# Cross-attention's row maxima: one instruction over two PSUM banks and one shift a head, in place of two of each

## The chip, the cores and the metric

One core of one Trainium2 chip runs the whole program. The metric is the device time of one execution in microseconds (us); the kernel before took 717.56 us, the median of three runs (717.15 to 718.02).

## The reference

Four batches of 256 tokens by 128 features, and a context of 512 rows by 256 features for each. The program is a cross-attention block followed by a transformer layer with a mixture of experts:

```
x = x + layernorm(xattn(layernorm(x), ctx)) ;  x = x + ffn_layer(layernorm(x))

xattn: q = x Wq (16 heads of 64);  k, v = split(ctx Wkv);  one learned null key and value put in front
       sim = (q / 8) k^T          per head: 256 queries x (512 keys + the null key)
       attn = softmax(sim);  out = (attn v) Wout, layernormed
ffn_layer: causal self-attention (16 heads of 8, 8 kv heads), then 8 experts of 448 hidden, top 2
```

The softmax takes each row's maximum over 512 scores and the null score, and subtracts it before the exponential. The change is to how that maximum and the shift made of it are computed.

## The kernel before, in words

**Stages.** `load_and_split` (to about 36 us of the trace), `cross_attention` (to about 395 us), then the residual, self-attention, routing and experts. Only `cross_attention` is touched. float32 products are made of three (or two) fp32r matmuls of high and low parts, so each tile that a matmul reads is rounded by ScalarE (the head) and has its remainder taken by VectorE (the tail).

**Tiling.** A head has two query tiles of 128 rows (t = 0, 1) against 512 keys, so one tile's scores are 128x512 float32 and fill one PSUM bank; tile t goes to `s_bank[t]`. There are 4 batches of 16 heads, 64 heads in all.

**Order.** Each engine has its own hand-written `steps(b, which)`. A step h works on several heads at once, in a software pipeline. FIRST (steps -4 to 1) fills it; BODY (steps 2 to 17) runs in a hardware loop three times, and once more, unrolled, for the last batch. In step h:

- VectorE (`steps`, L610): maximum of head h+2, tile 0 (L582); the q tail of head h+3 (L577); the shift of tile 0 (L587); the maximum and shift of tile 1; two tails of the transposed probabilities of head h (L606); the tails of the step's projection units (L122, L125 and L126, L129); the reciprocal of the sum (L592); the o tail (L598).
- ScalarE (L537): q head (L510), two heads of transposed probabilities (L534), a unit in `q_whole` if there is one (L107 to L112), the two exponentials of head h+2 (L516), the unit in `proj_bank`, the null exponential (L521), the o head (L527).
- TensorE (L479): eight transposes (L439), the units (L94, L96 or L87), `weighted_values` of h-1 (L451), `project_out` of h-2 (L460), `project_q` of h+4 (L414), `scores` of h+3 (L426).
- GpSimd (L645): d0, the total, p0 and the two normalised tiles `p_norm` (L657) of each head.

**Projection units.** The keys and values of a head pair or a token tile are projected just in time. `AT` (L357) gives each step its units: a key unit ("k": two tails of 64x512 on VectorE), a value unit ("v": one tail) or a context transpose ("c"). In each batch step 7 has a key unit in `q_whole` and a value unit in `proj_bank`; step 16 the same for the next batch; step 10 has the two context units, the first in `q_whole`. `q_whole` is the bank that q is projected into, so its unit waits for the step's q tail (L398).

**Waits that the change touches.** `scores` raises `s_ps` once a tile and waits until the exponential of the same tile of the head before is done (L424). `maximum(b, h, t)` waits for its own tile of scores (L581), `shift` for the maximum (L586), and `exponential` for its tile's shift through `bias_s` (L513). GpSimd's d0 waits for both shifts (L646). In the loop the waited values and the column of `s0n` (`null_score`, L367) depend on the loop's register.

Of the kernel before, what the change touches and what calls it, by code (L numbers as in the profile page):

```python
# [20 lines left out]
P = 128  # L21
# [293 lines left out]
def cross_attention(nc, k, dram):  # L315

    with ExitStack() as ctx:
# [20 lines left out]
        banks = [bank(f"bank{i}") for i in range(8)]  # L338
# [56 lines left out]
        def _(pe):  # L395
# [22 lines left out]
            def scores(b, h):  # L418
                pe.wait_ge(q_lo_s, b * H + h + 1)
                if h % 2 == 0:  # L420
                    pe.wait_ge(k.proj_lo, (b + h // H) * NU + UNITS.index(("k", h % H // 2)) + 1)
                for t in range(QT):
                    if h >= 1:
                        pe.wait_ge(p_exp, b * H * QT + QT * (h - 1) + t + 1)  # L424
                    for i, q in enumerate((q_hi, q_lo)):
                        last = pe.matmul(s_bank[t][:, :], q[:, h % 2, t * P:(t + 1) * P], keys[:, h % H, :],  # L426
                                         start=i == 0, stop=i == 1)
                    last.then_inc(s_ps, 1)
# [76 lines left out]
        def _(act):  # L505
# [6 lines left out]
            def exponential(b, h, t):  # L512
                act.wait_ge(bias_s, b * H * QT + QT * h + t + 1)  # L513
                if h >= 2:
                    act.wait_ge(p_norm_s, b * H * QT + QT * (h - 2) + t + 1)
                act.activation(p_raw[:, h % 2, t, :], s_bank[t][:, :], ACT.Exp,  # L516
                               bias=bias[:, h % H, t:t + 1], scale=X_SCALE, accum_out=row_sum[:, h % H, t:t + 1]).then_inc(p_exp, 1)
# [54 lines left out]
        def _(dve):  # L572
# [7 lines left out]
            def maximum(b, h, t):  # L580
                dve.wait_ge(s_ps, b * H * QT + QT * h + t + 1)  # L581
                dve.tensor_reduce(neg_max[:, h % H, t:t + 1], s_bank[t][:, :], AX_X, ALU.max, negate=True).then_inc(max_s, 1)  # L582

            def shift(b, h, t):

                dve.wait_ge(max_s, b * H * QT + QT * h + t + 1)  # L586
                dve.scalar_tensor_tensor(bias[:, h % H, t:t + 1], neg_max[:, h % H, t:t + 1], X_SCALE, null_score(b, h, t),  # L587
# [22 lines left out]
            def steps(b, which, last_batch=False):  # L610
                end = H if last_batch else which.stop + 3
                for h in which:
                    if 0 <= h + 2 < end:
                        maximum(b, h + 2, 0)
                    if 0 <= h + 3 < end:
                        q_tail(b, h + 3)
                    if 0 <= h + 2 < end:
                        shift(b, h + 2, 0)
                        maximum(b, h + 2, 1)
                        shift(b, h + 2, 1)  # L620
# [23 lines left out]
        def _(pool):  # L644
            def normalise_probs(b, h):  # L645
                pool.wait_ge(bias_s, b * H * QT + QT * (h + 1))  # L646
# [968 lines left out]
```

## Time and profile before

| what | value |
|---|---|
| timed runs: median (range) | 717.56 us (717.15 to 718.02) |
| profiled execution: span from first to last instruction | 711.4 us |
| its own time outside the span | not on the page; the span is 6.2 us under the timed median |
| cross-attention in the trace | 36 to 395 us |
| PE, PEld busy | 602.2 us (85%), 492.3 us (69%) |
| DVE (VectorE) busy | 587.9 us (83%), 1282 instructions |
| ACT (ScalarE) busy | 454.6 us (64%) |
| POOL (GpSimd) busy | 227.9 us (32%) |
| TensorE's granted clock, mean | 0.956 |

Busy shares are over the whole span. In the loop of cross-attention VectorE and TensorE are both close to nine tenths busy, so the shares alone don't say which waits decide; the chain of starts within one step does. A row of a timeline gives start, duration, engine, line, operation, and in brackets the idle time before it and who ended it. Instructions of one engine overlap a little (a 0.68 us reduction is followed by the next start 0.60 us later), so distances from start to start are used below.

### The profile page before, as it was taken

The page shows a single profiled execution, that of the slowest core. Times are in us where ns is not written, and L with a number is a line of the kernel's source. Part 1 is how long each engine was busy: PE and PEld are TensorE (multiplying, and loading weights), DVE is VectorE, ACT ScalarE, POOL GpSimd, SP SyncE. Part 2 cuts the span into 40 slices and gives each one's busy share as a digit, 9 for nine tenths or more (in the row PEclk, how much of TensorE's full clock was granted, in tenths as well). Part 3 has the DMA queues.
Part 4 walks back from the last instruction along what each step waited for, and adds up shares of the span by engine and source line. Part 5 has one row for each costly group of instructions (what it writes and reads, how often), then busy time and mean ns, then how long its engine had stood idle before and what let it go on. Part 6 is the DMA issues. An engine that isn't in the chain of part 4 may idle for free. (4 is left out here: it accounts for less than half of the span.)

```text
span 711.4 us, 13311 instructions
## 1 busy us (share of the span) xinstructions
PE 602.2 (85%) x3580; PEld 492.3 (69%) x3580; DVE 587.9 (83%) x1282; ACT 454.6 (64%) x1094; POOL 227.9 (32%) x435
## 2 busy tenths in 40 slices
PE   2979889988999999899999336899997689797996
PEld 2757778767887778778787325666666577575885
DVE  4768899878898788998889747899983599979995
ACT  3657777766777677767777125888883356344563
POOL 1553334323333333333335354722132321414000
PEclk9989999999999999999999868999998699998999
DMA  8020000000000000000000002000000220200000
GB/s 255 17 54 2 2 29 3 1 1 0 0 30 0 1 0 0 0 0 1 1 1 1 1 4 82 1 1 0 0 0 1 78 77 2 77 1 0 0 0 29
DMA packets 15342, 13.48 MB, mean 19 GB/s; under 512 B 1984, under 2 KB 14656, under 8 KB 15296
## 3 DMA queue, kind: packets, MB, share of 16 engines
q1 hardware_dynamic: 15072, 12.94, 6.2%
q8 instruction: 16, 0.26, 0.2%
q14 instruction: 30, 0.25, 0.1%
q10 hardware_dynamic: 224, 0.03, 0.0%
HBM read 12.44 MB, written 0.52 MB: 18 GB/s over the span
## 5 line engine op out<-in xcount | busy, mean ns | idle before, releaser
L516 ACT ACTIVATE p_raw<-bank,bias 128x512 f32<-128x512 f32 x128 | 87.7, 688 | 43.1 <-DVE bias L587 39.4
L582 DVE TENSOR_REDUCE neg_max<-bank 128x1 f32<-128x512 f32 x128 | 86.9, 679 | 5.9 <-issue 4.0
L657 POOL TENSOR_SCALAR p_norm<-p_raw,rinv 128x512 f32<-128x512 f32 x128 | 87.0, 692 | 0.1
L606 DVE TENSOR_TENSOR pT_lo<-bank,pT_hi 128x512 fp32r<-128x512 f32 x128 | 82.4, 685 | 3.9 <-issue 2.3
L534 ACT ACTIVATE pT_hi<-bank 128x512 fp32r<-128x512 f32 x128 | 69.7, 599 | 24.9 <-PE bank L439 23.4
L1472 ACT ACTIVATE act_hi<-act_f 128x512 fp32r<-128x512 f32 x56 | 35.4, 632 | 58.9 <-DVE act_f L1515 58.8
L439 PE MATMUL bank<-ident,p_norm 128*128 128x128 f32 x512 | 66.8, 273 | 0.4 <-DVE pT_lo L606 0.4
L439 PEld LDWEIGHTS bank<-ident,p_norm 128*128 128x128 f32 x512 | 59.8, 141 | 9.3 <-issue 1.2
L451 PE MATMUL bank<-pT_hi,vals 128*128 128x256 f32 x256 | 64.9, 286 | 1.5 <-DVE o_lo L598 1.5
L451 PE MATMUL bank<-pT_lo,vals 128*128 128x256 f32 x256 | 64.0, 283 | 0.0
L426 PE MATMUL bank<-keys,q_hi 128*128 128x512 f32 x128 | 54.7, 427 | 3.0 <-ACT p_raw L516 2.8
L426 PE MATMUL bank<-keys,q_lo 128*128 128x512 f32 x128 | 51.4, 401 | 0.0
L451 PEld LDWEIGHTS bank<-pT_hi,vals 128*128 128x128 f32 x256 | 48.4, 189 | 4.2 <-issue 1.1
L451 PEld LDWEIGHTS bank<-pT_lo,vals 128*128 128x128 f32 x256 | 48.6, 190 | 2.1
L1519 DVE TENSOR_TENSOR act_lo<-act_f,act_hi 128x512 fp32r<-128x512 f32 x56 | 47.2, 842 | 2.7 <-ACT act_hi L1472 1.4
L587 DVE SCALAR_TENSOR_TENSOR bias<-neg_max,s0n 128x1 f32<-128x1 f32 x128 | 41.5, 324 | 7.9 <-DVE neg_max L582 1.9
L650 POOL TENSOR_TENSOR total<-row_sum,e 128x2 f32<-128x2 f32 x64 | 12.5, 195 | 103.4 <-ACT e L521 103.4
L1515 DVE TENSOR_TENSOR act_f<-up_w,gate 128x512 f32<-128x512 f32 x56 | 45.2, 808 | 0.3
L1044 ACT ACTIVATE p_raw<-s_pair,neg_max 128x128 f32<-128x128 f32 (+1 forms) x128 | 43.0, 427 | 3.0 <-DVE neg_max L1109 3.0
L1507 DVE TENSOR_TENSOR up_w<-u_bank,wide 128x512 f32<-128x512 f32 x48 | 33.1, 689 | 8.8 <-PE u_bank L1420 7.4
L1109 DVE TENSOR_REDUCE neg_max<-s_pair 128x2 f32<-128x256 f32 x64 | 32.3, 545 | 5.7 <-PE s_pair L948 5.6
L1428 PE MATMUL d_bank<-act_hi,dn_hi 128*128 128x512 f32 x56 | 23.7, 423 | 15.3 <-DVE act_lo L1519 15.3
(272 smaller groups left out, 1731.3 us busy)
## 6 DMA issues: line engine op xcount, KB each, us to landing
ctx_raw<-in_ctx SPq DMA_DIRECT2D x4, 512.0 KB, 4.7
wkv_raw<-in_L_xattn_Wkv SPq DMA_DIRECT2D x2, 1024.0 KB, 11.1
gu_raw<-in_L_ffn_w_gate SPq DMA_DIRECT2D x4, 448.0 KB, 3.6
gu_raw<-in_L_ffn_w_up SPq DMA_DIRECT2D x4, 448.0 KB, 4.3
dn_raw<-in_L_ffn_w_down SPq DMA_DIRECT2D x4, 448.0 KB, 5.1
wout_raw<-in_L_xattn_Wout SPq DMA_DIRECT2D x2, 512.0 KB, 14.8
x<-in_x SPq DMA_DIRECT2D x1, 512.0 KB, 6.8
wq_raw<-in_L_xattn_Wq SPq DMA_DIRECT2D x1, 512.0 KB, 10.2
```

Source lines behind the costliest of these rows:

```text
L426: last = pe.matmul(s_bank[t][:, :], q[:, h % 2, t * P:(t + 1) * P], keys[:, h % H, :], start=i == 0, stop=i == 1)
L439: last = pe.transpose(t_bank[half][:, j * N + t * P:j * N + (t + 1) * P], p_norm[:, h % 2, t, kt * P:(kt + 1) * P], k.ident[:, :])
L451: last = pe.matmul(o_bank, vals[:, kt, h % H, :], x[:, h % 2, kt, :], start=kt == 0 and i == 0, stop=kt == KT - 1 and i == 1)
L516: act.activation(p_raw[:, h % 2, t, :], s_bank[t][:, :], ACT.Exp, bias=bias[:, h % H, t:t + 1], scale=X_SCALE, accum_out=row_sum[:, h % H, ...
L534: act.activation(pT_hi[:, h % 2, 2 * half:2 * half + 2, :], t_bank[half][:, :].rearrange("p (j n) -> p j n", j=2), ACT.Copy).then_inc(t_hi ...
L582: dve.tensor_reduce(neg_max[:, h % H, t:t + 1], s_bank[t][:, :], AX_X, ALU.max, negate=True).then_inc(max_s, 1)
L587: dve.scalar_tensor_tensor(bias[:, h % H, t:t + 1], neg_max[:, h % H, t:t + 1], X_SCALE, null_score(b, h, t), ALU.mult, ALU.min).then_inc( ...
L606: dve.tensor_tensor(pT_lo[:, h % 2, 2 * half:2 * half + 2, :], t_bank[half][:, :].rearrange("p (j n) -> p j n", j=2), f(pT_hi[:, h % 2, 2 ...
L657: pool.tensor_scalar(p_norm[:, h % 2, t, :], p_raw[:, h % 2, t, :], rinv[:, h % H, t:t + 1], 1.0, ALU.mult, ALU.mult).then_inc(p_norm_s, 1)
L1044: last = act.activation(p_raw[:, p % 4, j, t, 0:n], s_bank[(p % 2) * REP + j][:, t * N:t * N + n], ACT.Exp, bias=neg_max[:, t, REP * (p % ...
L1515: dve.tensor_tensor(act_f[:, n % 2, :], up_w[:, n % 2, :], gate[:, n % 2, :], ALU.mult).then_inc(mul_s, 1)
L1519: dve.tensor_tensor(act_lo[:, n % 2, :], act_f[:, n % 2, :], f(act_hi[:, n % 2, :]), ALU.subtract).then_inc(a_lo_s, 1)
```

## The change

The two score banks become one PSUM tensor `s_both` of 128 x 2 x 512, with `s_bank[t]` a view of each half. `maximum` reads both halves in one TENSOR_REDUCE with two outputs a partition and waits for both tiles' scores; one `shift` makes both biases; `max_s` and `bias_s` count heads instead of tiles. The q tail stays between maximum and shift.

```diff
-        banks = [bank(f"bank{i}") for i in range(8)]
+        s_both = ctx.enter_context(nc.psum_tensor("s_both", [P, QT, BANK], F32))
+        banks = [s_both[:, t, :] for t in range(QT)] + [bank(f"bank{i}") for i in range(2, 8)]
...
             def exponential(b, h, t):
-                act.wait_ge(bias_s, b * H * QT + QT * h + t + 1)
+                act.wait_ge(bias_s, b * H + h + 1)
...
-            def maximum(b, h, t):
-                dve.wait_ge(s_ps, b * H * QT + QT * h + t + 1)
-                dve.tensor_reduce(neg_max[:, h % H, t:t + 1], s_bank[t][:, :], AX_X, ALU.max, negate=True).then_inc(max_s, 1)
-
-            def shift(b, h, t):
-
-                dve.wait_ge(max_s, b * H * QT + QT * h + t + 1)
-                dve.scalar_tensor_tensor(bias[:, h % H, t:t + 1], neg_max[:, h % H, t:t + 1], X_SCALE, null_score(b, h, t),
+            def maximum(b, h):
+                dve.wait_ge(s_ps, b * H * QT + QT * (h + 1))
+                dve.tensor_reduce(neg_max[:, h % H, :], s_both[:, :, :], AX_X, ALU.max, negate=True).then_inc(max_s, 1)
+
+            def shift(b, h):
+
+                dve.wait_ge(max_s, b * H + h + 1)
+                dve.scalar_tensor_tensor(bias[:, h % H, :], neg_max[:, h % H, :], X_SCALE, null_score(b, h, 0, QT),
                                          ALU.mult, ALU.min).then_inc(bias_s, 1)
...
                     if 0 <= h + 2 < end:
-                        maximum(b, h + 2, 0)
+                        maximum(b, h + 2)
                     if 0 <= h + 3 < end:
                         q_tail(b, h + 3)
                     if 0 <= h + 2 < end:
-                        shift(b, h + 2, 0)
-                        maximum(b, h + 2, 1)
-                        shift(b, h + 2, 1)
+                        shift(b, h + 2)
...
             def normalise_probs(b, h):
-                pool.wait_ge(bias_s, b * H * QT + QT * (h + 1))
+                pool.wait_ge(bias_s, b * H + h + 1)
```

## Rows read from the trace of the kernel before

**Rows 1.** The page's costliest groups: busy, mean ns, idle before.

```profile
L582 DVE TENSOR_REDUCE neg_max<-bank 128x1 f32<-128x512 f32 x128 | 86.9, 679 | 5.9 <-issue 4.0
L587 DVE SCALAR_TENSOR_TENSOR bias<-neg_max,s0n 128x1 f32<-128x1 f32 x128 | 41.5, 324 | 7.9 <-DVE neg_max L582 1.9
```

**Rows 2.** Busy time by stretch, second loop iteration: PE, PEld, DVE, ACT, POOL, clock, DMA.

```profile
147.10:239.10 92.00, 83.44 (x525) 71.12 (x524) 80.32 (x172) 66.79 (x173) 30.75 (x80) 1.00 0.02 6
```

**Rows 3.** The waits, 60 to 400 us: total us, times, longest.

```profile
ACT p_raw L516 <- DVE bias L587: 35.3, 35, 1.6
...
DVE keys L125 <- ACT keys L110: 17.2, 29, 0.9
...
PE bank L94 <- DVE q_lo L577: 7.0, 7, 1.2
...
PE bank L87 <- DVE q_lo L577: 4.8, 3, 1.6
```

**Rows 4.** Timeline, all engines: from a maximum after a key unit to the next step's.

```profile
204.98 0.68 DVE L582 TENSOR_REDUCE neg_max<-bank 128x1 f32<-128x512 f32 x1
...
207.32 0.69 ACT L516 ACTIVATE p_raw<-bank,bias 128x512 f32<-128x512 f32 x1
...
208.62 0.69 DVE L129 TENSOR_TENSOR vals<-bank,vals 128x512 fp32r<-128x512 f32 x1
...
209.62 0.68 DVE L582 TENSOR_REDUCE neg_max<-bank 128x1 f32<-128x512 f32 x1
...
209.78 1.36 POOL L657 TENSOR_SCALAR p_norm<-p_raw,rinv 128x512 f32<-128x512 f32 x2
...
210.22 0.41 DVE L577 TENSOR_TENSOR q_lo<-bank,q_hi 128x256 fp32r<-128x256 f32 x1
...
210.55 0.60 DVE L587 SCALAR_TENSOR_TENSOR bias<-neg_max,s0n 128x1 f32<-128x1 f32 x1
...
211.18 0.69 ACT L516 ACTIVATE p_raw<-bank,bias 128x512 f32<-128x512 f32 x1 [0.74 <-DVE bias L587]
...
212.09 0.69 ACT L516 ACTIVATE p_raw<-bank,bias 128x512 f32<-128x512 f32 x1
```

**Rows 5.** Groups by shape: the self-attention's maxima, two outputs a partition.

```profile
L1109 DVE TENSOR_REDUCE neg_max<-s_pair 128x2 f32<-128x512 f32 x32 | 21.6, 675 | 0.0
...
L1109 DVE TENSOR_REDUCE neg_max<-s_pair 128x2 f32<-128x256 f32 x32 | 13.3, 414 | 5.7 <-PE s_pair L948 5.6
```

**Rows 6.** Timeline, back-to-back exponentials, after a unit in q_whole.

```profile
200.47 0.69 ACT L516 ACTIVATE p_raw<-bank,bias 128x512 f32<-128x512 f32 x1
...
201.13 0.70 ACT L516 ACTIVATE p_raw<-bank,bias 128x512 f32<-128x512 f32 x1
```

**Rows 7.** Timeline of a step with a key unit in q_whole (step 7).

```profile
175.76 0.41 DVE L577 TENSOR_TENSOR q_lo<-bank,q_hi 128x256 fp32r<-128x256 f32 x1
...
176.22 0.50 PE L94 MATMUL bank<-cT_hi,wkv_hi 128*128 128x512 f32 x1 [1.20 <-DVE q_lo L577]
...
177.92 0.59 ACT L109 ACTIVATE keys<-bank 64x512 fp32r<-64x512 f32 x1 [2.21 <-PE bank L94]
```

**Rows 8.** Timeline at the loop's turn, GpSimd quiet.

```profile
147.11 0.69 DVE L582 TENSOR_REDUCE neg_max<-bank 128x1 f32<-128x512 f32 x1 [2.13 <-issue]
...
148.05 0.15 DVE L587 SCALAR_TENSOR_TENSOR bias<-neg_max,s0n 128x1 f32<-128x1 f32 x1
...
149.24 0.69 ACT L516 ACTIVATE p_raw<-bank,bias 128x512 f32<-128x512 f32 x1 [0.15 <-DVE bias L587]
```

**Rows 9.** Timeline in the unrolled last batch, after a key step.

```profile
352.08 0.68 DVE L582 TENSOR_REDUCE neg_max<-bank 128x1 f32<-128x512 f32 x1
...
354.21 0.69 ACT L516 ACTIVATE p_raw<-bank,bias 128x512 f32<-128x512 f32 x1
```

**Rows 10.** Timeline of the first head's maximum.

```profile
39.03 0.69 DVE L582 TENSOR_REDUCE neg_max<-bank 128x1 f32<-128x512 f32 x1 [1.83 <-PE bank L426]
39.22 0.63 PE L426 MATMUL bank<-keys,q_lo 128*128 128x512 f32 x1
```

More of the change, by code:

```diff
@@ L425, in scores @@
                     for i, q in enumerate((q_hi, q_lo)):
-                        last = pe.matmul(s_bank[t][:, :], q[:, h % 2, t * P:(t + 1) * P], keys[:, h % H, :],
+                        last = pe.matmul(s_bank[t], q[:, h % 2, t * P:(t + 1) * P], keys[:, h % H, :],
                                          start=i == 0, stop=i == 1)
@@ L512, in exponential @@
             def exponential(b, h, t):
-                act.wait_ge(bias_s, b * H * QT + QT * h + t + 1)
+                act.wait_ge(bias_s, b * H + h + 1)
                 if h >= 2:
                     act.wait_ge(p_norm_s, b * H * QT + QT * (h - 2) + t + 1)
-                act.activation(p_raw[:, h % 2, t, :], s_bank[t][:, :], ACT.Exp,
+                act.activation(p_raw[:, h % 2, t, :], s_bank[t], ACT.Exp,
                                bias=bias[:, h % H, t:t + 1], scale=X_SCALE, accum_out=row_sum[:, h % H, t:t + 1]).then_inc(p_exp, 1)
```

## The prediction, made before the changed kernel was run

> **What bounds the kernel now.** I read the page's costliest groups first [rows 1]: 128 reductions of 679 ns and 128 shifts of 324 ns, a tiny operation that should not take that long. Then the busy time by stretch [rows 2]: in a loop iteration of 92.0 us VectorE is busy for 80.3 and TensorE for 83.4, so neither has much room. Then the waits [rows 3], which say more: VectorE itself waits 17.2 us in 29 key steps for ScalarE's rounding of the keys, and ScalarE waits 35.3 us for the bias. The two engines hand the work to and fro. Last the timeline of one step [rows 4]. Its chain is: maximum of tile 0 at 209.62, second exponential at 212.09. From a second exponential to the next maximum it is 207.32 to 209.62, 2.30 us, and that leg runs through ScalarE: L129 starts at 208.62, 1.30 after the exponential, as soon as ScalarE's value rounding behind that exponential is through. So the period is 2.30 + 2.47 = 4.77 us, and it is a cycle through both engines. VectorE's busy time alone doesn't set it. In a key step the second leg is longer, since two roundings of ScalarE follow the exponential and two tails follow them.
>
> The measure of the change is therefore **D, the distance from the start of a head's first maximum to the start of its second exponential.** D now: 2.47 after a value step (209.62 to 212.09), 2.34 after a key step in the loop (204.98 to 207.32) [rows 4], 2.13 at the loop's turn [rows 8] and 2.13 after a key step in the unrolled batch [rows 9].
>
> **Why the first shift is long.** In the loop it lasts 0.60 us (210.55 to 211.15) and it ends as GpSimd's pair of `p_norm` ends (209.78 + 1.36 = 211.14) [rows 4]; at the turn, with GpSimd quiet, it takes 0.15 [rows 8]. The shift reads two tensors of SBUF, and it is held until GpSimd lets go. The Trainium skill, "SBUF — State Buffer", section "SBUF: two separate sides", gives the rule: a VectorE operation with two SBUF inputs and a GpSimd one lock a shared port pair against each other, for a whole instruction. Were the shift long for another reason, such as the loop's register work, the new one would be long too, and each D below 0.45 us longer (some +25 us in all); the 0.15 row speaks against it.
>
> **The change, part by part.**
> 1. The reduction. The self-attention has the same operation with two outputs: 675 ns for 512 elements, 414 ns for 256 [rows 5], 1.02 ns an element. So 1024 elements: 679 + 522 = 1.20 us, against 2 x 0.679 now. The next start follows 0.60 after a 0.68 reduction (209.62 to 210.22), so the q tail now starts 1.12 after the maximum, 0.52 later than now. No row shows a read over two banks: the lower bound is 1.20, the upper 1.36 (nothing saved). I take 1.20, the nearer row by shape.
> 2. The shift. 0.33 after the q tail (210.22 to 210.55). There GpSimd is at 0.06 us from its end, or done, so I price it at 0.15 [rows 8] plus the 0.03 to the exponential (211.15 to 211.18). The two outputs cost nothing more by the rows of 5. The second shift and its wait for the maximum go.
> 3. The exponentials now run back to back: 0.66 from start to start [rows 6].
> New **D = 1.12 + 0.33 + 0.18 + 0.66 = 2.29 us**, whatever step came before. VectorE saves far more (it reaches the probabilities' tails 0.7 to 0.8 us earlier), but then it waits for ScalarE's keys or values, which hang on the second exponential. That saving is idle time and I cost it at nothing; its cover is the wait of [rows 3], which grows.
> 4. The q tail, 0.52 later. `project_q` and `scores` come later in TensorE's order and don't feel it. A unit in `q_whole` does: TensorE waits for q_lo before L94 in seven key-and-value steps and before L87 in three [rows 3]. In [rows 7] q_lo starts at 175.76, L94 at 176.22, ScalarE's key rounding at 177.92, and the exponentials stand behind that rounding. The whole chain moves by 0.52. So here the delay is on the path and no shorter D repays it.
> 5. The wait for both tiles' scores. [Rows 1] charge the 128 maxima with next to no wait for TensorE, so in mid-loop the scores are there in time; only after a q_whole unit do I count tile 1's as just due (+0.07, a guess of small weight). In the prologue they are late: the first maximum waits for TensorE until 39.03, and tile 1's last matmul runs from 39.22 for 0.63 [rows 10]. So it starts at 39.9.
> 6. Loop's turn: the maximum at 147.11 follows a 2.13 us stop that the trace puts down to VectorE's own issue [rows 8], and the scores were long done. VectorE may reach the loop's end up to 0.65 earlier, as the last step's tails hang on its own order. The new D costs 2.29 - 2.13 = 0.16 against that: between +0.16 and -0.5; I take -0.3.
> GpSimd's d0 starts sooner and nobody waits for it. No DMA and no queue is moved.
>
> **The sum** (us):
> - 15 loop steps after a value step or the double one: 15 x (2.29 - 2.47) = -2.7, and +0.2 for late scores of tile 1.
> - 12 loop steps after a key step: 12 x (2.29 - 2.34) = -0.6.
> - 7 steps with a key unit in q_whole: 7 x 0.52 = +3.6.
> - 3 steps with context units: between 0 and 0.52 each, as TensorE's next wait there (a tail behind the probabilities) comes earlier; I take +0.2, so +0.6.
> - 2 turns and the exit: 3 x -0.3 = -0.9.
> - The unrolled batch: 4 steps after a key step, 4 x 0.16 = +0.6, and a few others, +0.2 in all.
> - The prologue: 0.3 to 0.9 for the first two heads' tile 1, less 0.3 regained: +0.8.
> Sum: **+1.8 us**. On the profiled execution the span goes from 711.4 to 713.2; what lies outside the span (6.2 us to the median) doesn't change, so the median goes from 717.56 to 719.4. A measurement of this kernel can tell about 0.2%, 1.4 us, from no change. The forecast is just above that.
>
> **The rivals.**
> - *The freed VectorE time pays.* If the period were VectorE's own work, each of some 55 steps would lose 0.7 us or more until TensorE binds: in [rows 2] TensorE is busy 83.4 of 92.0, so at most 8.6 an iteration, with the last batch some 30 in all; at half that, -17, 700 us. For it: VectorE's idle time in value steps is nearly nil. Against it: VectorE's waits for ScalarE in 29 key steps [rows 3]. Chance 0.07. The Trainium skill, "VectorE: DVE Perf Modes", section "Rules for kernel authors", leans the same way: it says to keep the number of chained operations down.
> - *The loop's own costs fall further: faster.* Place: ScalarE's and VectorE's sequencers in the 48 looped heads, which compute registers for every wait and shift. D after a key step is 2.34 in the loop and 2.13 in the unrolled batch [rows 4, 9], and the two differ only in that register work. If the merged chain sheds 0.06 more a head, -2.9; with 0.65 at each turn instead of 0.3, -1.1; and a prologue that costs nothing, -0.8: 719.4 - 4.8 = 714.6. It decides from 0.03 us a head up. For it: that difference. Against: the turn's D, in the loop too, is 2.13 [rows 8], so most of it may be GpSimd's hold. Chance 0.22.
> - *A read over two banks costs as two reads: slower.* The maximum takes 1.36, D is 2.45, and 39 steps with the seven, the three and four of the prologue pay 0.16: +8.5, 727.9. From 1.25 us on it decides the sign beyond doubt. For it: no row of a read over two banks. Against: the linear price of [rows 5]. Chance 0.15.
> - *Nothing moves*, delays and gains cancel: 717.6. Chance 0.06.
>
> **How the numbers follow.** The forecast, 719.4, has 0.50, with a range of its own of 717 to 722; of it 0.28 lies more than 1.4 us above 717.56 and 0.22 within. The loop rival gives 0.20 to faster and 0.02 to the middle, the first rival 0.07 to faster, the third 0.15 to slower, the last 0.06 to the middle. That makes faster 0.27, within 0.2% 0.30, slower 0.43. The range of 713.5 to 726 leaves out the first rival, most of the third, and a little below.
>
> **What would show it in the changed profile.** L582 becomes 64 reductions near 1.20 us (1.36: the third rival). L587 becomes 64 shifts near 0.16, so VectorE's busy time falls by some 10 + 31 = 41 us to about 547, and its wait for keys L110 grows from 17 to over 30 us. The exponentials stand 0.66 apart everywhere. D is 2.29 after key and value steps alike. TensorE's waits for q_lo before L94 and L87 grow by about 0.5 a time, ten times. The end of cross-attention moves by +2, and what follows keeps its length. The prediction is wrong if the wait for keys L110 doesn't grow, if the new shift is still held, or if TensorE's granted clock in the loop leaves the 1.00 of [rows 2].

## The result, and the profile after

The changed kernel took **723.43 us** (median of 4 runs, 722.95 to 723.95) beside 717.79 us (717.15 to 718.73) of the kernel before in the same comparison: ratio 1.0089, 95% interval 1.0070 to 1.0109. It is slower by 5.6 us, where +1.8 was forecast; 723.43 lies inside the range of 713.5 to 726. In the profiled execution of after the span is 721.0 us (its own time 722.95), TensorE's mean granted clock 0.947.

VectorE's totals came close to the forecast. The first fence is the page's line of the engines, the second VectorE's groups by line from 36 to 400 us with the two changed lines (the answer to [rows 1]), the third the waits from 60 to 400 us (the answer to [rows 3]).

```profile
PE 606.8 (84%) x3580; PEld 495.8 (69%) x3580; DVE 551.5 (76%) x1154; ACT 451.6 (63%) x1094; POOL 228.6 (32%) x435
```

```profile
L583 DVE TENSOR_REDUCE neg_max<-s_both 128x2 f32<-128x1024 f32 x64 | 77.9, 1217 | 4.7 <-PE s_both L427 4.1
...
L588 DVE SCALAR_TENSOR_TENSOR bias<-neg_max,s0n 128x2 f32<-128x2 f32 x64 | 10.2, 160 | 0.0
```

```profile
ACT p_raw L517 <- DVE bias L588: 44.3, 41, 1.8
...
DVE keys L125 <- ACT keys L110: 44.2, 29, 1.7
...
PE bank L94 <- DVE q_lo L578: 10.2, 7, 1.5
...
PE bank L87 <- DVE q_lo L578: 6.7, 3, 2.2
```

VectorE is busy 36.4 us less (551.5 against 587.9), and its wait for ScalarE's keys has grown by 27.0 us in the same 29 steps: the saved time stands there as idle time. TensorE's waits for q_lo are longer in the same seven and three places. In the second loop iteration VectorE is now busy 70.2 us, TensorE 83.6:

```profile
148.80:240.30 91.50, 83.59 (x527) 71.47 (x526) 70.22 (x140) 65.95 (x172) 30.84 (x82) 1.00 0.02 6
```

The timeline of after, of a step behind a value unit (the answer to [rows 4]):

```profile
211.89 0.69 DVE L129 TENSOR_TENSOR vals<-bank,vals 128x512 fp32r<-128x512 f32 x1 [0.89 <-ACT vals L112]
...
212.89 1.21 DVE L583 TENSOR_REDUCE neg_max<-s_both 128x2 f32<-128x1024 f32 x1
...
214.02 0.41 DVE L578 TENSOR_TENSOR q_lo<-bank,q_hi 128x256 fp32r<-128x256 f32 x1
214.35 0.15 DVE L588 SCALAR_TENSOR_TENSOR bias<-neg_max,s0n 128x2 f32<-128x2 f32 x1
...
214.61 0.69 ACT L517 ACTIVATE p_raw<-s_both,bias 128x512 f32<-128x512 f32 x1 [0.90 <-DVE bias L588]
...
215.29 0.68 ACT L517 ACTIVATE p_raw<-s_both,bias 128x512 f32<-128x512 f32 x1
```

D, from the first maximum to the second exponential, is 2.40 (212.89 to 215.29). The shift takes 0.15 and is not held. The leg from the second exponential to the next maximum is 2.30 as before.

**Where the 5.6 us lie.** I read D and the leg of all 64 heads in both traces and added up the differences (after minus before). They come to +5.5 us at the start of the last head's maximum (386.00 to 391.53), about the difference of the medians. The spans differ by 9.6 us (711.4 to 721.0). The other 4.1 lie in later stages, whose source is the same: 3.8 in the experts (557.2 to 706.3 us before, 563.0 to 715.9 after), where TensorE's granted clock was 0.95 in before and 0.92 in after. What follows the last head's maximum takes between 325.4 us (before) and 332.5 us (e1) in the traces of this case, so medians can't be compared as finely as the starts of the heads.

| place | forecast | measured |
|---|---|---|
| first four heads (pipeline fill) | +0.8 | +2.8 |
| loop steps without a unit in q_whole | -3.1 | -1.0 |
| 7 steps with a key unit in q_whole | +3.6 | +4.3 |
| 3 steps with context units | +0.6 | +2.5 |
| 2 turns and the exit | -0.9 | -4.1 |
| unrolled batch | +0.8 | +1.0 |
| sum | +1.8 | +5.5 |

The forecast's direction was right, and four of its six terms were mis-sized. In the first head the merged maximum waits for the fourth scores matmul, and in the next for slow ones (timeline of after, answer to [rows 10]; here TensorE is granted 0.78 of its clock on average, from 38.0 to 53.8 us, and 0.76 in the kernel before, from 37 to 51):

```profile
40.07 1.23 DVE L583 TENSOR_REDUCE neg_max<-s_both 128x2 f32<-128x1024 f32 x1 [1.64 <-PE s_both L427]
...
43.85 0.72 PE L427 MATMUL s_both<-keys,q_hi 128*128 128x512 f32 x1
...
44.37 0.63 PE L427 MATMUL s_both<-keys,q_lo 128*128 128x512 f32 x1
...
45.03 1.23 DVE L583 TENSOR_REDUCE neg_max<-s_both 128x2 f32<-128x1024 f32 x1 [0.68 <-PE s_both L427]
```

The seven steps go as written. In step 7 (answer to [rows 7]) L94 starts 1.60 after the maximum, and the whole chain behind it moves, D from 4.66 to 5.19:

```profile
177.42 1.21 DVE L583 TENSOR_REDUCE neg_max<-s_both 128x2 f32<-128x1024 f32 x1
178.55 0.41 DVE L578 TENSOR_TENSOR q_lo<-bank,q_hi 128x256 fp32r<-128x256 f32 x1
...
179.02 0.50 PE L94 MATMUL bank<-cT_hi,wkv_hi 128*128 128x512 f32 x1 [1.46 <-DVE q_lo L578]
...
180.71 0.59 ACT L109 ACTIVATE keys<-bank 64x512 fp32r<-64x512 f32 x1 [2.47 <-PE bank L94]
```

And the turn (answer to [rows 8]) has lost its stop. VectorE goes from the last step's o tail straight to the next maximum:

```profile
148.33 0.42 DVE L599 TENSOR_TENSOR o_lo<-bank,o_hi 128x256 fp32r<-128x256 f32 x1
148.88 1.22 DVE L583 TENSOR_REDUCE neg_max<-s_both 128x2 f32<-128x1024 f32 x1
```

The leg there fell from 4.46 to 1.87 us (second turn: 4.24 to 1.83), while D rose from 2.13 to 2.80. Two shorter stops of 0.4 us before L606 in each iteration of before, put down to "issue" as well, are gone too. So the delays cost 10.6 us, the ordinary loop steps gave 1.0 back, and 4.1 came from a place where the change was not meant to act. Even of that 1.0 the shorter D is only 0.4. Another 0.8 is the leg ahead of step 7 (2.53 to 2.29 us, three times), from which one of the two shorter stops has gone, and other legs take 0.2.

### The profile page after: what moved, and what is told of

It reads as the page before. It is cut to its first block and busy times, and to the rows that moved or that the text cites. A ratio compares the mean times of both kernels' runs of the same rounds, so it can differ in the third digit from the quotient of the medians.

```text
span 721.0 us, 13039 instructions
## 1 busy us (share of the span) xinstructions
PE 606.8 (84%) x3580; PEld 495.8 (69%) x3580; DVE 551.5 (76%) x1154; ACT 451.6 (63%) x1094; POOL 228.6 (32%) x435
## 5 line engine op out<-in xcount | busy, mean ns | idle before, releaser
L517 ACT ACTIVATE p_raw<-s_both,bias 128x512 f32<-128x512 f32 x128 | 87.0, 686 | 50.3 <-DVE bias L588 49.7
L583 DVE TENSOR_REDUCE neg_max<-s_both 128x2 f32<-128x1024 f32 x64 | 77.9, 1217 | 4.7 <-PE s_both L427 4.1
L427 PE MATMUL s_both<-keys,q_hi 128*128 128x512 f32 x128 | 55.0, 430 | 2.7 <-ACT p_raw L517 2.6
L125 DVE TENSOR_TENSOR keys<-bank,keys 64x512 fp32r<-64x512 f32 x29 | 19.8, 684 | 44.2 <-ACT keys L110 44.2
L427 PE MATMUL s_both<-keys,q_lo 128*128 128x512 f32 x128 | 51.4, 401 | 0.0
L1514 DVE TENSOR_TENSOR act_f<-up_w,gate 128x512 f32<-128x512 f32 x56 | 48.6, 869 | 0.4 <-DVE act_lo L1518 0.2
L1518 DVE TENSOR_TENSOR act_lo<-act_f,act_hi 128x512 fp32r<-128x512 f32 x56 | 44.5, 794 | 2.6 <-ACT act_hi L1471 1.6
L1465 ACT ACTIVATE gate<-g_bank 128x512 f32<-128x512 f32 x56 | 32.6, 583 | 8.0 <-PE u_bank L1419 8.0
## 6 DMA issues: line engine op xcount, KB each, us to landing
wq_raw<-in_L_xattn_Wq SPq DMA_DIRECT2D x1, 512.0 KB, 10.2
```

The lines of the kernel that those rows point to most:

```text
L427: last = pe.matmul(s_bank[t], q[:, h % 2, t * P:(t + 1) * P], keys[:, h % H, :], start=i == 0, stop=i == 1)
L517: act.activation(p_raw[:, h % 2, t, :], s_bank[t], ACT.Exp, bias=bias[:, h % H, t:t + 1], scale=X_SCALE, accum_out=row_sum[:, h % H, t:t + ...
L583: dve.tensor_reduce(neg_max[:, h % H, :], s_both[:, :, :], AX_X, ALU.max, negate=True).then_inc(max_s, 1)
L1514: dve.tensor_tensor(act_f[:, n % 2, :], up_w[:, n % 2, :], gate[:, n % 2, :], ALU.mult).then_inc(mul_s, 1)
L1518: dve.tensor_tensor(act_lo[:, n % 2, :], act_f[:, n % 2, :], f(act_hi[:, n % 2, :]), ALU.subtract).then_inc(a_lo_s, 1)
```

## The experiments

"End" in the table is the start of the last head's maximum: 386.0 in before, 391.5 in after. Theory A: the merged instruction costs what it delays (q_lo, and the first heads, which wait for both tiles), and the turn's gain comes from something apart from it, the fetching of VectorE's instructions in a long loop body. Rival B: D itself sets the time, and the turn is the merge's own gain. The ratio to before is taken with runs of before in the same comparison. There were four of these, and before's median in them was 716.38 (e1 to e4), 716.82 (e6 to e9), 717.86 (e10, e11) and 718.55 us (e12, e13).

| kernel | median us (lowest, highest; runs) | ratio to before, 95% | end |
|---|---|---|---|
| e1_qfirst | 714.67 (708.62, 718.06; 10) | 0.9965 [0.9933, 0.9997] | 383.1 |
| e2_pad | 731.77 (730.29, 732.09; 4) | 1.0207 [1.0171, 1.0244] | 398.8 |
| e3_before_qfirst | 716.42 (712.39, 719.17; 10) | 0.9987 [0.9961, 1.0013] | 384.8 |
| e4_before_ptr | 708.29 (705.08, 708.92; 4) | 0.9865 [0.9822, 0.9908] | 377.6 |
| e6_ptr_qfirst | 706.49 (706.18, 707.58; 4) | 0.9869 [0.9842, 0.9896] | 374.9 |
| e7_merge_best | 710.57 (708.47, 714.84; 10) | 0.9922 [0.9897, 0.9948] | 377.7 |
| e8_pad16 | 723.71 (723.14, 725.37; 4) | 1.0117 [1.0086, 1.0148] | 391.4 |
| e9_two_max_one_shift | 732.83 (732.25, 733.33; 4) | 1.0235 [1.0207, 1.0264] | 399.2 |
| e10_ptr_lean | 704.78 (701.67, 706.12; 6) | 0.9816 [0.9779, 0.9854] | 371.9 |
| e11_before_lean | 714.23 (710.99, 719.38; 12) | 0.9963 [0.9936, 0.9991] | 381.4 |
| e12_before_front96 | 718.24 (714.05, 722.96; 12) | 0.9991 [0.9963, 1.0020] | 386.2 |
| e13_ptr_front96 | 707.20 (704.65, 710.27; 6) | 0.9861 [0.9831, 0.9892] | 374.5 |

Six medians lie outside what I had expected by my theory: e1, e2, e3, e9, e10 and e11 (each expectation is printed below). In all six, what was looked for is in the trace, and the sum of what it gives or costs was off.

### The price of the delayed q tail

**e1_qfirst**: after, with the q tail ahead of the merged maximum in the steps that have a unit in q_whole (7, 10 and 16).

```diff
+                    q_first = any(src is q_whole for _, src in units(h, last_batch))
+                    if q_first and 0 <= h + 3 < end:
+                        q_tail(b, h + 3)
                     if 0 <= h + 2 < end:
                         maximum(b, h + 2)
-                    if 0 <= h + 3 < end:
+                    if not q_first and 0 <= h + 3 < end:
                         q_tail(b, h + 3)
```

> The change, with the q tail moved in front of the maximum in the ten steps that have a unit in q_whole (steps 7, 10 and 16). Theory (the q tail delayed by the long reduction holds TensorE's unit, ScalarE's rounding and both exponentials): L94 starts 0.46 us after q_lo starts and q_lo now leads the maximum, so a key-and-value step's maximum-slot to second exponential falls from 5.2 to about 4.1 us, seven times (-7.7), the context steps from 3.5 to about 2.7, three times (-2.5), and the third context step's TensorE at half clock goes too (-1.2): 723.4 falls to 711 to 714. Rival (those steps are bound by VectorE's own tails or by ScalarE, the q tail only looks late): under 2 us change, 721 to 723.

714.67 us, 8.8 less than after (the ratios to before, 0.9965 and 1.0089, say the same). Step 7 in its timeline:

```profile
176.61 0.41 DVE L578 TENSOR_TENSOR q_lo<-bank,q_hi 128x256 fp32r<-128x256 f32 x1
176.94 1.22 DVE L583 TENSOR_REDUCE neg_max<-s_both 128x2 f32<-128x1024 f32 x1
...
177.08 0.49 PE L94 MATMUL bank<-cT_hi,wkv_hi 128*128 128x512 f32 x1 [0.34 <-DVE q_lo L578]
...
178.77 0.59 ACT L109 ACTIVATE keys<-bank 64x512 fp32r<-64x512 f32 x1 [1.34 <-PE bank L94]
```

D there is 3.73 instead of 5.19 and the maximum starts 0.33 later, since the tail is ahead of it, so one such step gains 1.1 us net. The reduction now runs beside L94. Against after, the seven steps give 10.2 and the three context steps 4.1 us, and the legs take 3.9 and the first four heads, which the edit doesn't reach, 1.9 back. So the position of one 0.41 us tail was worth more than the whole change. It also shows that the order, and not the merge, made these steps dear.

**e3_before_qfirst**: the same edit on before.

> The kernel before, with only the q tail moved in front of the first maximum in steps 7, 10 and 16. Theory: the chain of those steps begins 0.60 us earlier, seven times fully (-4.2) and three times for 0.3 (-0.9): 717.6 falls to 712 to 713.5. Set against e1 it gives the price of the merge without its delay of the q tail. Rival (q_lo isn't what those steps wait for): within 1 us of 717.6.

716.42 us, not told from before (0.9987, interval across 1) and not the 712 to 713.5 that I expected. The rival's number came, but not for its reason, since those steps do wait for q_lo. The seven steps' D falls from 4.66 to 3.73 and the three context steps' from 2.99 to 2.06, 9.3 us together. But 5.2 us come back in the legs around them, 1.4 in the D of the steps behind, and 1.6 in the first four heads, which the edit doesn't reach. Between its slowest and fastest run lie 6.8 us, so a gain of 1 us (1.2 at the end) can't be told here.

### What the turn's stop hangs on

**e2_pad**: after, with four memsets of one element per head in VectorE's loop body, 64 in all; the body has 312 instructions again, as in before, instead of 248 (VectorE's records of one iteration in the trace, without those of semaphores).

```diff
...
                         probs_tail(b, h, 1)
+                    if which is BODY and not last_batch:
+                        for _ in range(4):
+                            dve.memset(scratch[:, 4 * (h - 2) + _:4 * (h - 2) + _ + 1], 0.0)
```

> The change, with 64 tiny memsets of a scratch tile added to VectorE's loop body (four a step, behind the probabilities' tails, where VectorE waits 0.9 us or more), so that its loop is about as long as before (some 312 instructions instead of 248). Theory (the stop of 2.13 and 1.92 us at the loop's turn before was the refetch of a body too long to stay resident, and the change removed it): the turn's issue stop of about 2 us comes back twice, instruction packets rise from 19 to about 30, and the time rises by 3 to 5 us to 726.5 to 728.5. Rival (the stop went because VectorE waits elsewhere or comes earlier): no stop at the turn, packets stay near 19, time within 1 us of 723.4.

731.77 us, 8.3 more than after, where I had expected 3 to 5. Its 64 memsets an iteration cost nothing where they stand (the ordinary steps' D and legs are after's to 0.02 us on average, but for the leg ahead of step 7). Of the end's +7.3 us, 6.5 lie at the two turns and 0.7 in the leg ahead of step 7, which is back at 2.5 us. The first turn:

```profile
148.61 0.42 DVE L600 TENSOR_TENSOR o_lo<-bank,o_hi 128x256 fp32r<-128x256 f32 x1
152.87 1.23 DVE L584 TENSOR_REDUCE neg_max<-s_both 128x2 f32<-128x1024 f32 x1 [3.83 <-issue]
```

**e8_pad16** has one memset per head (264 instructions), **e9_two_max_one_shift** is after with the reduction cut in two again around the q tail and one shift (280):

```diff
-            def maximum(b, h):
-                dve.wait_ge(s_ps, b * H * QT + QT * (h + 1))
-                dve.tensor_reduce(neg_max[:, h % H, :], s_both[:, :, :], AX_X, ALU.max, negate=True).then_inc(max_s, 1)
+            def maximum(b, h, t):
+                dve.wait_ge(s_ps, b * H * QT + QT * h + t + 1)
+                last = dve.tensor_reduce(neg_max[:, h % H, t:t + 1], s_both[:, t, :], AX_X, ALU.max, negate=True)
+                if t == 1:
+                    last.then_inc(max_s, 1)
...
```

> The kernel after with one memset of one element per head in the loop's body on VectorE (16 more, 264 instructions; it was 248, and 312 with four per head, which put the stop at the turn back). If what stays resident ends at 256 instructions, the turns cost 2 to 4 us more each and the queue of instructions shows about 25 packets or more: 728 to 730 us. If it ends above 264, the turns keep 1.85 us and 19 packets and the time is within 1.5 us of the kernel after's 723.4. Were it the memsets' own time that made the padded kernel slow (64 at 0.06 us in the loop), a quarter of them would give a quarter of it, +2 us, spread over the heads and not at the turns.

> The kernel after with its reduction cut in two again (tile 0, the tail of the queries, tile 1) and still one shift. By the rows: 0.60 + 0.33 + 0.60 + 0.15 and the 0.26 and 0.68 us up to the second exponential, with 0.1 us of starts: 2.65 to 2.75 us from the first maximum to the second exponential (2.40 in the kernel after), but 4.66 instead of 5.20 in the seven steps with the whole query bank, and the first heads no longer wait for the second tile's scores. Loop's body is 280 instructions on VectorE, between the 248 that stayed resident and the 312 that did not. If 280 still fits, the turns keep their 1.85 us and 19 packets of instructions, and the time is 725 to 731 us; if not, the two turns cost 3 us more each, the packets go to 25 to 30, and it is 731 to 737.

Neither has the stop: the legs at the turns are 1.86 and 1.83 in the one, 1.88 and 1.83 in the other. e8 took 723.71 us, as after. In e9, D is 2.69, as worked out, and 4.65 in the seven steps; this costs 10.9 us in the ordinary loop steps and gives back 5.4 in the ten with q_whole. 732.83 us is the slowest of all, 1.8 above what I expected for a body that fits: one shift for two maxima that are still apart only makes the first exponential wait for both. So the merged shift without the merged reduction is worse than either kernel.

**e11_before_lean** turns this round: before, with all its reductions, shifts and tails, and only fewer register instructions (a body of 264). Each wait of the loop against another value costs VectorE one; semaphores of their own for the two tiles and halves let one value serve several waits.

```diff
+        max1_s = sem("max1_s")
+        t1_hi_s = sem("t1_hi_s")
...
-            def maximum(b, h, t):
-                dve.wait_ge(s_ps, b * H * QT + QT * h + t + 1)
+            def maximum(b, h, t, one_wait):
+                if not one_wait or t == 0:
+                    dve.wait_ge(s_ps, b * H * QT + QT * h + (QT if one_wait else t + 1))
...
-                dve.wait_ge(max_s, b * H * QT + QT * h + t + 1)
+                dve.wait_ge((max_s, max1_s)[t], b * H + h + 1)
...
-                dve.wait_ge(t_hi_s, b * 2 * H + g + 1)
+                dve.wait_ge((t_hi_s, t1_hi_s)[half], b * H + h + 1)
```

> The kernel before, all its VectorE and ScalarE work kept, with 48 fewer register instructions in VectorE's loop body (264 instead of 312): the two tiles' maxima have a semaphore each and so share the value they are waited for by, the two halves' copies of the transposed probabilities too, and in the loop one wait for both tiles' scores stands ahead of the first maximum. If it is the length of the body that costs the stop at the turn, the two turns lose 2 to 3 us each (legs of 4.46 and 4.24 us to about 1.9), the stops at the tail of the probabilities go, the packets of instructions fall from 30 to 19 or 20, and the time is -4 to -6 us: 711 to 713. Rival: it is the merged instruction itself that shortens the turn; then nothing moves, 717.

714.23 us, ratio 0.9963 [0.9936, 0.9991], the end 4.6 us earlier. The median gives less than the 4 to 6 us that I expected, since D at the turn grows. The first turn's leg is 1.83 us:

```profile
143.77 0.39 DVE L603 TENSOR_TENSOR o_lo<-bank,o_hi 128x256 fp32r<-128x256 f32 x1
144.09 0.67 DVE L586 TENSOR_REDUCE neg_max<-bank 128x1 f32<-128x512 f32 x1
145.61 0.42 DVE L580 TENSOR_TENSOR q_lo<-bank,q_hi 128x256 fp32r<-128x256 f32 x1 [0.85 <-ACT q_hi L512]
```

The two turns' legs lose 5.0 us, 1.8 of it comes back as D, since the q tail now waits for ScalarE. That is after's gain at the turn (5.0 and 1.3) without its merge: rival B falls, and the turn belongs to the body of instructions, not to the merge.

**e12_before_front96** and **e13_ptr_front96** ask whether it is the length or the place in the program. They put 96 memsets at the very front of VectorE's program, ahead of its wait for x.

```diff
...
         def _(dve):
+            for i in range(96):
+                dve.memset(scratch[:, i:i + 1], 0.0)
             dve.wait_ge(x_in, 16)
```

> The kernel before with 96 memsets of one element at the very front of VectorE's program, while it waits for x (to 7.5 us). The loop's body keeps its 312 instructions and only lies 96 further back: counted from VectorE's first instruction it ran from the 77th to the 389th, now from the 173rd to the 485th. So far the bodies that ended at 317, 333, 341 and 353 had no stop at the turn and those that ended at 381 and 389 had one; by these runs length and place can't be told apart. Theory of the length: 312 is too long wherever it lies, the stops of about 2 us stay, and the time is 717 to 718 us. Theory of the place: what matters is how many blocks of fetched instructions the body touches, and a body moved back touches one fewer; then both turns lose 2 to 2.5 us, as in the shortened body, and the time is 713 to 714. Theory of the end: a loop that ends behind the 360th or so is not kept; then the stops stay or grow. The Trainium skill, "Runtime: NRT & Kernel Launch", section "Instruction fetch mechanics", has 512 instructions in blocks of 256 at most at hand and a stall for a branch to outside them, which speaks for the place; no run so far shows either number.

> The same 96 memsets in front of the kernel with the null score as per-partition scalar and the tail of the queries first (706.5 us, with the stops at the turn). By the theory of the place the turns give their 3 us again: 702 to 705 us, beside 704.8 of the kernel with the shortened body. By the theory of the length it stays at 706 to 707.

718.24 and 707.20 us, beside 718.55 of before in the same comparison and 706.49 of e6: nothing moved. In e12 (VectorE's timeline; the two turns) the stops are there:

```profile
147.19 0.69 DVE L585 TENSOR_REDUCE neg_max<-bank 128x1 f32<-128x512 f32 x1 [2.35 <-issue]
...
239.46 0.69 DVE L585 TENSOR_REDUCE neg_max<-bank 128x1 f32<-128x512 f32 x1 [2.55 <-issue]
```

My theory of the place was wrong for this shift. The small stops of 0.4 us did move with it, from steps 6 and 17 to the first step of an iteration. The queue that carries instructions agrees with the stops, kernel by kernel. Its lines on the pages (packets, MB, share) are of before, after, e2, e11 and e12, in this order, one fence each:

```profile
q14 instruction: 30, 0.25, 0.1%
```

```profile
q14 instruction: 19, 0.16, 0.1%
```

```profile
q14 instruction: 30, 0.25, 0.1%
```

```profile
q14 instruction: 20, 0.16, 0.1%
```

```profile
q14 instruction: 31, 0.25, 0.1%
```

Bodies of 248, 264 and 280 instructions need 19 or 20 packets, those of 312 need 30 to 32. Where they fall says more than their number. From 130 to 344 us, a stretch that holds both turns, the view of before's DMA queues has twelve of them (first fence), and that of after has no such line. One of the twelve falls between 144.5 and 147.3 us, into before's first stop (second fence):

```profile
q14 instruction: 12, 0.10, 0.2%
```

```profile
q14 instruction: 1, 0.01, 1.2%
```

e8, e9 and e11 have none from 132 to 325 us either. So the shorter bodies went through their last two iterations without a fetch, and the stop at the jump back is time in which instructions are fetched again: shown is that it comes with the body of 312 and the packets in the loop, at both of its places. The Trainium skill, "Runtime: NRT & Kernel Launch", section "Instruction fetch mechanics", says that a taken branch to a target outside the stretch at hand forces a fetch before execution goes on; the trace agrees, at 1.9 to 3.8 us a time. Its figure of 512 instructions at hand, in blocks of 256, is not borne out as such: a body of 312 was not kept here at either place. Two things stay untested. Every body without a stop also ended at the 353rd instruction of VectorE's program or before, and every one with a stop at the 381st or later, so my third theory, of the place where the body ends, predicts the same; a short body far back would tell. And one move of 96 is one other place, not every one. What the exact bound is, and why the stop is 3.8 us in e2 and 2.1 in before, stays open too.

### The first shift's hold, and the first heads

**e4_before_ptr**: before, with the null score given to the shift as its per-partition scalar, so that it reads one SBUF tensor and a pointer instead of two tensors.

```diff
-                dve.scalar_tensor_tensor(bias[:, h % H, t:t + 1], neg_max[:, h % H, t:t + 1], X_SCALE, null_score(b, h, t),
-                                         ALU.mult, ALU.min).then_inc(bias_s, 1)
+                dve.tensor_scalar(bias[:, h % H, t:t + 1], neg_max[:, h % H, t:t + 1], X_SCALE, null_score(b, h, t),
+                                  ALU.mult, ALU.min).then_inc(bias_s, 1)
```

> The kernel before, with each shift as a TENSOR_SCALAR that reads the null score as its per-partition scalar instead of as a second SBUF tensor; the same values. Theory (the first shift is held by GpSimd's p_norm because it reads two SBUF tensors): the first shift falls from 0.60 to about 0.16 us, the distance from first maximum to second exponential in the loop from 2.47 and 2.34 to about 2.1, and the time falls by 4 to 9 us to 709 to 714. Rival (the hold has another cause, or a pointer operand is held too): shifts as long as before, time within 1 us of 717.6.

708.29 us, ratio 0.9865 [0.9822, 0.9908]. Its timeline:

```profile
206.25 0.68 DVE L582 TENSOR_REDUCE neg_max<-bank 128x1 f32<-128x512 f32 x1
206.40 1.37 POOL L657 TENSOR_SCALAR p_norm<-p_raw,rinv 128x512 f32<-128x512 f32 x2
206.84 0.41 DVE L577 TENSOR_TENSOR q_lo<-bank,q_hi 128x256 fp32r<-128x256 f32 x1
207.18 0.20 DVE L587 TENSOR_SCALAR bias<-neg_max,s0n 128x1 f32<-128x1 f32 x1
...
207.41 0.69 ACT L516 ACTIVATE p_raw<-bank,bias 128x512 f32<-128x512 f32 x1 [0.29 <-DVE bias L587]
...
208.38 0.69 ACT L516 ACTIVATE p_raw<-bank,bias 128x512 f32<-128x512 f32 x1 [0.19 <-DVE bias L587]
```

The shift takes 0.20 us in the middle of GpSimd's 1.37 us of `p_norm`, where it took 0.60 in [rows 4]. D is 2.13 behind most value and key steps (2.53 in step 9, 2.42 in step 17), and the ordinary loop steps' D is 7.6 us less in all. This confirms what the prediction read from [rows 4, 8]: the first shift was held by GpSimd. It is also the sharpest comment on the change: the merge freed the shift only by putting it behind `p_norm`, at D = 2.40; an operand of another kind frees it where it stands.

**e7_merge_best**: after, with e1's edit, and with maxima and shifts made tile by tile (own semaphores `max0_s`, `bias0_s`) in the first four heads and in the unrolled batch.

```diff
+                    by_tile = which is FIRST or last_batch
...
+                        tile_maximum(b, h + 2, 0) if by_tile else maximum(b, h + 2)
...
+                        tile_shift(b, h + 2, 0)
+                        tile_maximum(b, h + 2, 1)
+                        tile_shift(b, h + 2, 1)
```

> The kernel after, with tile-by-tile maxima and shifts in the first four heads and in the batch written out behind the loop, and with the tail of the queries first in the steps with the whole query bank. If the merged maximum costs there because each waits for the scores of the second tile (1.64, 0.93, 0.68, 0.19 us of wait in the first four) the fourth head comes 2 to 3 us sooner than in the kernel after, and the batch behind the loop keeps before's 2.13 us; the loop keeps the short turn, since its body is unchanged: 710 to 713 us. Rival: the first heads are late for the clock of TensorE that was granted there, not for the merge; then the fourth head stays within 1 us of after's and the time is that of the kernel with the tail first, 714.7 us.

710.57 us. The fourth head's maximum is at 51.18, 2.6 us before after's 53.80 and 0.2 from before's 50.95, at the same mean granted clock of 0.76 as before over that stretch. So the first heads were late for the merge's wait for both tiles. The unrolled batch's D gives 0.8 us more.

**e6_ptr_qfirst** has e4's and e1's edits on before; **e10_ptr_lean** adds e11's shorter body.

> The kernel before with both of the edits that were tried on it apart: the shift reads the null score as its per-partition scalar, and the tail of the queries stands ahead of the first maximum in the steps whose unit for the keys is made in the whole query bank. If the two act on different parts (the shift's wait on GpSimd's hold of the port, and the queries' tail on TensorE's chain in seven steps and three), the first gives -8 us again and the second -1 to -3: 705 to 707 us. The heads after key and value steps: 2.13 us from the first maximum to the second exponential, steps 7 and 16 about 3.7. Rival: what the tail in front gives was already eaten by the next steps (there it moved the end by 1 us only), then 708 us as with the first edit alone.

> The shorter loop body (264), the shift with its null score as per-partition scalar, and the tail of the queries first where the keys are made in the whole bank, all on the kernel before. If the three act on different parts, 706.5 us less the two turns' 4 to 6: 701 to 703 us. Rival: the padded turn is covered by something that is late next (there the first maximum then waits for ScalarE's copy or the exponentials), and only 1 to 2 us come: 705.

706.49 us: of the q tail's edit 2.7 us are left at the end of cross-attention, but the ratios to before don't tell e6 from e4 (0.9869 and 0.9865). e10: 704.78 us, ratio 0.9816 [0.9779, 0.9854], the end 14.1 us before before's and 3.1 before e6's. It has the lowest median here, 1.8% under before and 2.6% under after, though its interval meets e6's. It misses the 701 to 703 us expected, and the rival's 705 came: what the turn gives is late elsewhere. The turns give 5.1 us and hand 1.7 back; at the other end of the chain the ordinary D falls by 4.1 and the legs take 3.9.

## Why the prediction was right, and where its terms were off

- **The reduction and the shift** (points 1 and 2) were sized well: 1.217 us against 1.20, 0.160 against 0.15. The rival "a read over two banks costs as two" (1.36) is out.
- **D** was 2.40 in the loop against the forecast's 2.29. The maximum to q_lo took 1.13 (1.12 forecast) and q_lo to shift 0.33 (0.33); from the shift's start to the exponential 0.26 instead of 0.18, and 0.68 instead of 0.66 between the exponentials. The 0.18 was put together from two rows, the turn's shift and the 0.03 behind a held one; the unrolled batch of after has it (351.60 to 351.78), the loop has 0.08 more. So after's loop steps gained 0.07 behind a value step and lost 0.07 behind a key step: their D gave 0.4 us in all, and with the legs 1.0, where 3.1 was forecast. This is one of the steps that failed, an error of 0.11 us in the distance that sets every ordinary step.
- **The count of those steps** was wrong too. The sum has 15 and 12 loop steps; the trace has 18 behind a value step or a double one, 15 behind a key step, 3 behind the context step and the loop's first, 37 in all. (The third rival's 39 are these and the two turns.) At the prediction's own D of 2.29, set against before's 2.47, 2.34, 2.53 and 2.57 in these four groups, the 37 would give -5.0 (an estimate), not -3.3, and the whole forecast would have been about +0.1, no change. So the sign of the forecast rested in part on a miscount.
- **"That saving is idle time"**: right. The wait for keys went from 17.2 to 44.2 us, and the leg behind the exponentials kept its 2.30 and 3.85.
- **The seven steps**: 0.52 forecast, 0.54 measured in D, and 0.08 more in the leg.
- **The three context steps** were mis-sized at 0.2 each. "TensorE's next wait there comes earlier" was wrong: L87 gates ScalarE's rounding as L94 does, and D grew by the full 0.53. The third grew by 0.93 and its leg by 0.66. TensorE had stood idle for 2.24 us before L87 in all three (1.59 in before), and only after this one its granted clock fell to 0.52 for 3.4 us, one level down (from 2.4 to 1.2 GHz). Timeline and busy time by stretch of after:

```profile
289.24 1.90 PE L87 MATMUL bank<-ident,ctx_raw 128*128 128x128 f32 x8 [2.24 <-DVE q_lo L578]
```

```profile
289.20:292.60 3.40, 3.36 (x16) 3.37 (x17) 1.86 (x3) 2.28 (x6) 0.20 (x1) 0.52 0.00 0
```

- **The first heads**: the forecast took 0.3 to 0.9 for "the first two heads' tile 1, less 0.3 regained". It was +1.0 at the first maximum, +0.8 and +1.3 in the next two heads and nothing regained but 0.3. The step that failed priced tile 1's scores from one row at the first head; in the second they take 0.72 and 0.63 a matmul, and each following head hangs on the one before. e7 settles the cause.
- **The turns**: "between +0.16 and -0.5; I take -0.3" had the mechanism wrong. I saw the 2.13 us stop in [rows 8] and treated it as a constant of the loop, though it was a wait of 2 us that nobody was named for, and the diff shortened that loop by 64 instructions. It measured -1.8 a turn (leg -2.5, D +0.7). e2 and e11 settle that the merge is not its cause. Without this gift, 3.7 us at the turns and 0.8 ahead of step 7, after would have been about 10 us slower than before, near 728 us and outside the range of 713.5 to 726; e2's end (398.8) shows it with a still longer stop. That the median fell inside the range is luck in this part: a gain that was not understood covered delays priced too low.
- **"What lies outside the span (6.2 us)"** was read wrongly. After's span lies 1.95 us under its own time, and a run of before with a span of 716.9 took 718.74. With the same 1.8 us the profiled execution of before would have taken 713.2 us (an estimate), less than any timed run of before on record (714.08 and more), so most of the 6.2 is that this execution was a short one. The forecast is a difference and doesn't depend on it.
- **"What follows keeps its length"** didn't hold in the two traces (4.1 us more in later stages, at a lower granted clock in the experts); by the range over all traces this is no effect that can be put down to the change.
- **What would make it wrong** named TensorE's clock leaving 1.00 in the loop; it did so at that one place.
- **The rivals.** "The freed VectorE time pays" didn't happen. "The loop's own costs fall further" named the right place, the sequencers, for the wrong reason: a register's cost per head didn't fall, D in the loop (2.40) stays over the unrolled 2.33, and the stop at the turn fell instead.

By the end of cross-attention the +5.5 us hence are: 6.8 us for the delayed q tail in ten steps (1.1 of them at a lower clock), 2.8 for the first heads' wait for both tiles, 1.0 in the unrolled batch, less 1.0 in the ordinary loop steps and 4.1 at turns and exit.

## What to carry to other kernels

Merging two instructions saves the engine's time at once, but the kernel's only if that engine's time is on the chain; what the longer instruction makes late (the work queued behind it, and the first result that used to go out alone) has to be priced at every place where someone waits for it. When a tiny operation is long, look at what holds it before merging it away: here the operand's kind was worth 8 us and the merge cost 6. And count the instructions of a loop body: a stop "issue" at the jump back, with more packets in the instruction queue, can be bought off with fewer register instructions (here 48 of 312, and 0.4% of the time, interval 0.1% to 0.6%).

## What the runs showed of the hardware that was not expected

- VectorE's loop bodies of up to 280 instructions were kept (no packet of instructions from 132 to 325 us in e8, e9 and e11), and those of 312 were fetched again, at 1.9 to 3.8 us a turn; moving such a body 96 instructions back left its stops at the turns.
- The same 2.24 us of idle TensorE was followed by a fall of the granted clock in one of three places in after, and in another of the three in e8 (0.50 over 197.7 to 201.1, where after kept 1.00).
- A reduction of 128x1024 over two PSUM banks took 1.217 us: 0.54 for its second 512 elements, close to the 0.52 that [rows 5] give inside one bank.
